# Loading the next image in seven column blocks, one per unit, instead of in one transfer, in a fused convolution and attention kernel

## What is computed

```python
# layer 0: an inverted bottleneck with ternary weights and batch statistics
out = relu(batchnorm(conv(x, ternarize(w1)), g1, b1))                              # 1x1, 96 -> 576
out = relu(batchnorm(conv(out, ternarize(w2), pad=1, groups=576), g2, b2))         # 3x3 depthwise
out = batchnorm(conv(out, ternarize(w3)), g3, b3)                                  # 1x1, 576 -> 96
x = out + x
# layer 1: tokens (32, 3136, 96)
t = t + attention_by_fft(layernorm(t))
t = t + quantized_ffn(layernorm(t))
```

## Time and profile before

| what | value |
|---|---|
| median of 3 executions | 5265.94 us |
| lowest and highest of them | 5251.65 and 5277.84 us |
| the profiled execution's own time | 5252.71 us |
| its span, first to last instruction | 5250.9 us |
| busy share of PE, DVE, ACT, POOL | 91%, 68%, 65%, 49% |
| granted TensorE clock, mean | 0.958 |
| the convolution stage in it | about 280 to 1880 us |

### The profile page before, as it was taken

How to read it: one execution, slowest core, us unless ns; L and a number is a source line. 1 busy time by engine, 2 the same in 40 slices (tenths; PEclk the granted TensorE clock), 3 DMA queues, 4 the chain that set the end, 5 groups by cost and what they waited for, 6 DMA issues and landing times.

```text
span 5250.9 us, 153775 instructions
## 1 busy us (share of the span) xinstructions
PE 4775.0 (91%) x63188; PEld 3204.1 (61%) x63188; DVE 3551.9 (68%) x6475; ACT 3387.4 (65%) x5511; POOL 2574.2 (49%) x1508
## 2 busy tenths in 40 slices
PE   8989999999999989999678888888898898889886
PEld 8955555555555544444356666666666666666663
DVE  1156776776778766777427777777777777777776
ACT  4455655565566568888447667676677676777663
POOL 0067777777777756666323333333333333334331
PEclk9989999999999999999769999999999999999997
DMA  7656776777777689999556676776776766776762
GB/s 159 164 144 178 192 182 181 192 183 182 191 185 186 172 315 415 412 419 418 212 146 176 182 183 176 190 182 180 188 187 178 187 182 179 193 184 181 188 156 64
DMA packets 505463, 1072.16 MB, mean 204 GB/s; under 512 B 182240, under 2 KB 330240, under 8 KB 471872
## 3 DMA queue, kind: packets, MB, share of 16 engines
q1 hardware_dynamic: 504768, 1062.33, 70.7%
HBM read 557.40 MB, written 484.44 MB: 198 GB/s over the span
## 4 chain that ended last, share of the span: by engine, by line
PE 31%; DVE 8%; DMA 6%; issue 4%; ACT 2%; SPq 1%; POOL 0%; DVEq 0%; POOLq 0%; ACTq 0%
PE bank_w_s L1456 6%; DMA bt<-a_scratch 4%; PE bank_o L1434 3%; PE bank_w_s L1465 3%; PE bank_x L1409 3%; PE bank_c L1417 3%; PE bank_c L1418 2%; PE bank_c L1424 2%; PE bank_x L1406 2%; PE bank_l L1333 2%; PE bank_l L1390 1%; PE bank_o L1445 1%; DVE zq L1693 1%; PE bank_l L1349 1%; DVE wz L1794 1%
## 5 line engine op out<-in xcount | busy, mean ns | idle before, releaser
L772 POOL TENSOR_TENSOR hlo<-h,hhi 128x1682 f16<-128x1682 f32 x288 | 977.6, 3394 | 376.8 <-DVE hhi L825 376.8
L785 DVE BATCH_NORM_STATS2 stats<-z 128x6 f32<-128x392 f32 x1152 | 597.1, 560 | 437.9 <-ACT z L725 427.8
L735 ACT ACTIVATE h<-c1ps,s 128x1568 f32<-128x1568 f32 x288 | 479.3, 1664 | 629.3 <-PE c1ps L651 629.3
L683 PE MATMUL dwps<-hhi,taps 64*64 64x392 f16 x13824 | 692.9, 331 | 9.5 <-issue 9.4
L683 PE MATMUL dwps<-hlo,taps 64*64 64x392 f16 x13824 | 684.5, 328 | 4.4 <-issue 4.4
L1649 POOL TENSOR_TENSOR s_plus<-d_minus,imag_scaled 128x448 f32<-128x448 f32 (+1 forms) x192 | 203.6, 1060 | 897.1 <-ACT imag_scaled L1516 897.1
L1658 POOL TENSOR_TENSOR onat<-tb,o 96x448 f32<-96x448 f32 x224 | 262.7, 1173 | 643.3 <-DVE o L1718 643.3
L930 ACT ACTIVATE z2m<-z2m,s 128x784 f32<-128x784 f32 x512 | 489.5, 1029 | 104.0 <-DMA z2m<-z_scratch 103.4
L954 POOL TENSOR_TENSOR h_split<-z2m,h_split 128x1568 f16<-128x1568 f32 x128 | 405.2, 3166 | 264.6 <-DVE h_split L993 264.6
L683 PEld LDWEIGHTS dwps<-hhi,taps 64*64 64x64 f16 x13824 | 381.1, 106 | 251.1 <-issue 104.9
L683 PEld LDWEIGHTS dwps<-hlo,taps 64*64 64x64 f16 x13824 | 406.4, 106 | 185.3 <-issue 7.3
(11 more groups left out here) (234 smaller groups left out, 10110.9 us busy)
## 6 DMA issues: line engine op xcount, KB each, us to landing
z_scratch<-z SPq DMA_DIRECT2D x1152, 196.0 KB, 3.3
z2m<-z_scratch SPq DMA_DIRECT2D x64, 1960.0 KB, 15.9
z2m<-z_scratch SPq DMA_DIRECT2D x64, 1568.0 KB, 11.5
a_scratch<-a SPq DMA_DIRECT2D x896, 96.0 KB, 1.9
bt<-a_scratch SPq DMA_DIRECT2D x96, 672.0 KB, 6.5
t_scratch<-y SPq DMA_DIRECT2D x32, 1344.0 KB, 6.4
c_scratch<-cc SPq DMA_DIRECT2D x128, 336.0 KB, 3.7
d<-c_scratch SPq DMA_DIRECT2D x128, 336.0 KB, 3.9
```

The lines of the kernel that those rows point to most:

```text
L683: ins = nc.tensor.matmul(dw[64 * j:64 * j + 64, r, g, 0:QN], taps[half, u, da, dx, :, :].rearrange("p y c -> p (y c)"), part[half, s, a0:a ...
L735: nc.scalar.activation(to, src, ACT.Relu, bias=s1[:, 1, u:u + 1], scale=s1[:, 0, u:u + 1]).then_inc(h_ready, 1)
L772: nc.gpsimd.tensor_tensor(to, h, hi, ALU.subtract).then_inc(lo_ready, 1)
L785: nc.vector.bn_stats(stats[:, i, v, at:at + 6], z2[:, v % 3, g, r, :]).then_inc(s_stat, 1)
```

## The change

The one load of an image becomes seven loads of 448 columns each, issued in seven units one after the other: units 1 to 7 of SP's order for `m` = 0 and units 8 to 14 for `m` = 1. Only the first of the seven has the wait for the old image's split. The semaphore `ldx[m]` now counts seven transfers for each image (16 each), so ACT's wait before the first piece is for `j * 16 * NCH + 16`: all seven pieces of image `j`, the 16 being the image loaded in one transfer before the stage, which is unchanged.

```diff
         def xhi_scalar(act, j, m, c):
             if c == 0:
-                act.wait_ge(ldx[m], j * 16 + 16)
+                act.wait_ge(ldx[m], j * 16 * NCH + 16)
...
-                    if more and v in (1, 8):
-                        m = v // 8
-                        sp.wait_ge(xlo_ready, (2 * i + m + 1) * (NCH + 1))
-                        sp.dma_start(xin[:, m, :], x[2 * i + 2 + m]).then_inc(ldx[m], 16)
+                    if more and 1 <= v <= 2 * NCH:
+                        m, c = divmod(v - 1, NCH)
+                        if c == 0:
+                            sp.wait_ge(xlo_ready, (2 * i + m + 1) * (NCH + 1))
+                        cols = slice(c * CH, c * CH + CH)
+                        sp.dma_start(xin[:, m, cols], x[2 * i + 2 + m, :, cols]).then_inc(ldx[m], 16)
                     if v >= 2:
                         store_z2(sp, i, v - 2)
```

## The result

| | before | after |
|---|---|---|
| median of 8 executions | 5264.56 us | 5227.92 us |
| lowest to highest | 5251.65 to 5277.84 | 5210.75 to 5245.05 |
| profiled execution | 5252.71 | 5225.18 |
| its span | 5250.9 | 5223.1 |

The ratio after to before is 0.9936, with a 95% interval of 0.9919 to 0.9953. The kernel became faster by 0.64%, 36.6 us by the medians, where 30 us were forecast. The interval reaches from 25 to 43 us.

A forecast was written before the change was run, and what follows sets the result against it. TensorE's line of matmuls was taken to bound the convolution stage. From the profiled execution, 5252.7 - 30 + 0 + 0 = 5222.7, plus 13.2 for the median, gave 5236 us; range 5220 to 5262, the forecast's own 5224 to 5248.

The forecast's parts named there:

- -30 us: Convolution stage: gain expected from all TensorE stops on "issue" going away, with bounds of -20 and -31 us.
- The block for TensorE sat behind the load's packets: Convolution stage: claimed cause of the 18 stops, 20.0 us in all; TensorE's stored instructions ran out while its next block waited.
- bursts of 1176 KB: Convolution stage: the 30 whole-image loads removed, each 9.1 us from issue to landing; their removal was to bring -30 us.
- the upper end: Stage gain taken as 30 us, within bounds of 20 (idle time alone) and 31 (with the clock lost after stops).
- The added issues: 180 more load issues on SP, 0.43 to 0.59 us each, 77 to 106 us in all, hidden in SP's waits: zero cost.
- The moved end of the load: An image's last piece is issued later, 6.8 us before ACT reads it; zero cost up to a landing of 8.6 us.
- Rival D: Image loads: small transfers land late, ACT and then TensorE wait; slower, 5302 us at a 13 us landing; chance 0.04.
- The waits for `place_low`: TensorE's waits in the stage for the low parts that `place_low` copies: expected to stay near 6.5 us, ±3.
- rival C: Convolution stage: the waits for `place_low` go as well, -6.5 us more, near 5229 us; chance 0.03.
- Rivals A: Convolution stage: the stops only shrink, half of the 30 us stays, about 5251 us; chance 0.12.
- B: Convolution stage: the stops have nothing to do with the load's size and stay, 5266 us; chance 0.06.

The follow-up runs named there:

- e3: The 30 image loads of the convolution stage left out, against the changed kernel: no stops, stage 1534.4 us, whole execution 5243.15 us.
- e1: Changed kernel with all seven 168 KB pieces of an image issued together at unit 1 or 8: no stops, stage 1533.3 us, 0.9952 of before.
- e8: Changed kernel with two 588 KB halves per image in place of seven pieces, issued together at unit 1 or 8: stops 20.7 us, stage 1564.4 us.
- e4: Changed kernel with two 588 KB halves per image in place of seven pieces, issued three units apart: stops 1.8 us, stage 1534.8 us.
- e5: Changed kernel with six 196 KB blocks of 16 partitions per image, all issued together at unit 1 or 8: stops 49.8 us, stage 1601.5 us.
- e2: Changed kernel with six 196 KB blocks of 16 partitions per image in place of seven column pieces, one per unit: no stops, stage 1535.9 us.
- e9: Changed kernel with four 294 KB quarters per image in place of seven pieces, issued together at unit 1 or 8: stops 0.9 us, stage 1537.1 us.
- e10: The kernel before, run once more unchanged: stops 22.1 us, stage 1565.6 us, whole time 5241.76 us.
- e11: The changed kernel, run once more unchanged: no stops, stage 1533.2 us, whole time 5233.42 us.

## Why the prediction was right

- **What bounds.** TensorE's line of matmuls did: the stage lost 29.8 us where "-30 us" stood, and the distance forecast as about 1533 us was 1533.3.
- **The cause.** "The block for TensorE sat behind the load's packets" held in its main point: every stop ends just behind a late block, and without the load there is no stop (e3). My reason for the removed term, "bursts of 1176 KB", was too coarse. e1 keeps the burst of 1176 KB and has no stop, so the spreading over units, which is half of the change, was not needed. Time between the transfers counts: the same two halves give 20.7 us of stops together (e8) and 1.8 us three units apart (e4), and the same six row blocks 49.8 us (e5) and none (e2). That it is also the time of issuing that spares e1 and e9 is my reading and is not shown: within a burst the number of transfers and the time of issuing grow together (the seven issues of e1 take SP 0.56 us each), and no run varies one alone.
- **The size of the term.** I took the upper end over the 20 us of idle time, and that was right: 29.8 by distance. My reason for the difference was only partly right. The profile before has just two stretches at half clock in the stage, each costing about 1.7 us by the clock of its windows (0.74, 0.50 and 0.91 from 400 to 406 us). Of the 10.9 us that are neither `place_low` nor idle time, the clock explains 3.4. After the change 1.6 us of this kind are left. The other 6 us or so seem to go with the stops, some 0.3 us each; the profile has no name for them.
- **The added issues.** Sized too small and still free: 0.73 us each in place of 0.43 to 0.59, so 180 x 0.73 = 131 us; SP's spare time fell from 767 to 607 us.
- **The moved end of the load.** No wait of ACT for a load appears; the longest landing is 5.8 us where the price began at 8.6. Rival D had its point too far off to be reached.
- **The waits for `place_low`** stayed, 6.0 us against 6.5, so rival C did not come. Rivals A and B fell with the empty list of issue waits.
- **The whole time.** The median moved by 36.6 us where the stage gives 30 to 32. The interval holds both, and e10 and e11 show parts that no edit touches moving by 6 to 11 us between executions. I don't explain the 6.6 us further.

Three things stay open. The first is whether, within a burst, the number of transfers or the time of issuing is what helps. Second, the arithmetic of depth counts the load alone, not the stores around it, and it does not place e4: its halves leave some 410 KB, less than e9's 610, yet it has 1.8 us of stops against 0.9, and a landing of 5.8 us against 5.0. The landing times put all runs but e5 in order (none up to 4.4 us, 0.9 and 1.8 us of stops at 5.0 and 5.8, twenty and more from 7.0). e5, with a landing of 6.3 us, has the most stops of all; its slow draining may be why. Third, where exactly the block waits, in a queue with the load or for a share of the same DMA engines, was not tried; the profile does not show DMA engines one by one.

## What to carry to other kernels

An idle time of TensorE with the reason "issue" in the middle of a matmul stream is worth a look at the instruction queue in the same microseconds. If no block moved there, look for a transfer of about a megabyte issued earlier (the stops before begin 7 to 10 us behind the issue of a load), and cut it into four or more transfers. How fast the loop uses up instructions matters as well. From 1900 to 5250 us this kernel has transfers of 1344 KB and more, too, but a block lands only every 15.5 us in the middle, and the waits of TensorE there name "issue" once, for 0.7 us. Cut along columns: the blocks of 16 partitions of e5 drained more slowly and made the stops worse. And compare such edits by the length of the stage, which repeated to under 3 us here, where whole executions differed by 20.

## What the runs showed of the hardware

- Behind a transfer of 1176 KB two instruction blocks landed up to 10.5 us apart instead of 5.4. TensorE, at 128 matmuls and 128 weight loads per 5.39 us, outlived distances of up to 7.2 us after and of up to 8.4 us before without a stop. The shortest that went with a stop before was 7.7 us.
- The Trainium skill, in "Runtime: NRT & Kernel Launch", section "Instruction fetch mechanics", calls the fetch hidden. The 20.0 us of stops before say otherwise, and none was left with seven pieces or without the load (after, e1, e3).
- The Trainium skill, in "DMA: Bandwidth & Descriptors", section "Bandwidth", asks for transfers of 1 MiB and more. Here seven of 168 KB issued together landed 3.5 us after their issue each. That puts all of them within about 7.4 us where the issuing took 3.92 us (an estimate, the sum of the two), while the one of 1176 KB took 9.1: the small ones were not slower.
- Stops of about 2 us cost TensorE its clock in some places and not in others. In the stage before, the granted clock is 0.50 (1.2 GHz) after the stops that end at 400.43 us (2.19 us long) and 441.77 us (1.78 us), and 1.00 after the longer one that ends at 941.55 us (2.65 us). The runs don't tell what decides. The windows after the last two, columns as in the earlier trace rows:

```profile
442.00:444.00 2.00, 2.00 (x26) 1.11 (x28) 0.10 (x1) 1.72 (x2) 1.60 (x1) 0.50 0.97 227
943.00:945.00 2.00, 2.00 (x56) 1.36 (x48) 0.00 (x0) 2.00 (x5) 0.04 (x1) 1.00 0.68 218
```
